# Repeating B for a group's first tile earlier on TensorE, and wider spacing of three small attention steps

## What the reference computes

```
def step(h, inp):                       # layers 0 and 1, 4096 steps, 4 orders, 192 channels, 16 states
    u_t, dt_t, B_t, C_t = inp
    h = jnp.exp(dt_t[..., None] * A) * h + (dt_t * u_t)[..., None] * B_t[:, :, None, :]
    y = jnp.einsum('bkdn,bkn->bkd', h, C_t)
    return (h, y)

attn = jnp.einsum('bhnd,bhmd->bhnm', q, k) * D ** (-0.5)     # layers 2 and 3: no softmax
y = jnp.einsum('bhnm,bhmd->bhnd', attn, v)
return y.transpose(0, 2, 1, 3).reshape(B, N, E) @ Wff + bff
```

## Time and profile before

| what | value |
|---|---|
| median of 3 runs | 11526.75 us (11501.28 to 11531.94) |
| profiled execution | 11522.77 us, its span 11520.9 us |
| DVE busy | 10175.8 us (88%) |
| POOL busy | 9737.9 us (85%) |
| PE busy | 8853.6 us (77%), granted clock 0.739 on average |
| ACT busy | 6996.5 us (61%) |

### The profile page before, as it was taken

One profiled execution on the slowest core, in us unless ns is written; L12 is line 12 of the kernel. 1 busy time (PEld: TensorE's weight loads), 2 busy tenths in 40 slices (PEclk: granted clock), 3 DMA queues, 4 the chain that ended last, 5 costly groups with the idle time before them and its releaser, 6 DMA issues.

```text
span 11520.9 us, 94504 instructions
## 1 busy us (share of the span) xinstructions
PE 8853.6 (77%) x26272; PEld 2221.2 (19%) x26272; DVE 10175.8 (88%) x6086; ACT 6996.5 (61%) x10714; POOL 9737.9 (85%) x4231
## 2 busy tenths in 40 slices
PE   6876677876888667869777787788788877777757
PEld 2211111211112111212112121122111221122213
DVE  3899998999889998989999899899988999898873
ACT  4665555665556555667556765566755666567654
POOL 3899988899888998989988888888888888998860
PEclk8875577875778667769677796788677876777766
DMA  3666688666775565655776668956687565665550
GB/s 100 143 136 135 140 154 153 150 136 142 159 154 147 131 159 148 157 131 142 171 157 146 133 149 151 161 146 141 137 162 150 140 151 138 160 159 120 123 137 14
DMA packets 1781801, 1631.73 MB, mean 142 GB/s; under 512 B 1323982, under 2 KB 1325296, under 8 KB 1781276
## 3 DMA queue, kind: packets, MB, share of 16 engines
q1 hardware_dynamic: 1781276, 1625.69, 63.9%
HBM read 625.58 MB, written 194.51 MB: 71 GB/s over the span
## 4 chain that ended last, share of the span: by engine, by line
PE 22%; DVE 21%; issue 20%; POOL 20%; ACT 8%; SPq 4%; DMA 3%; DVEq 0%; POOLq 0%; ACTq 0%
POOL pr L1645 14%; DVE hs L1566 9%; DVE ps L1551 7%; DVE hs L1562 4%; PE ps L1032 4%; PE ps L861 3%; PE ps L826 3%; PE ps L1019 3%; PE ps L1010 2%; POOL bup L1659 2%; PE ps L994 2%; POOL dur L1659 2%; POOL us L1636 2%; ACT dec L1289 2%; SPq L720 1%
## 5 line engine op out<-in xcount | busy, mean ns | idle before, releaser
L1645 POOL TENSOR_TENSOR pr<-hs,crep 128x1024 f32<-128x1024 f32 x3072 | 7184.8, 2355 | 1202.5 <-PE ps L1032 587.2
L1566 DVE TENSOR_TENSOR_SCAN hs<-dec,carry,ps 128x1024 f32<-128x1024 f32 x1728 | 4054.2, 2346 | 232.6 <-POOL pr L1645 7.0
L1551 DVE TENSOR_TENSOR ps<-ps,dur 128x1024 f32<-128x1024 f32 x2304 | 2789.4, 1211 | 524.1 <-PE ps L1019 384.0
L1019 PE MATMUL ps<-sbc,selb 96*128 96x512 bf16 x4608 | 1842.0, 492 | 1788.5 <-DVE hs L1566 1240.2
L1289 ACT ACTIVATE dec<-dtr,ac 128x1024 f32<-128x1024 f32 x2304 | 2610.7, 1136 | 436.5 <-DVE hs L1566 424.4
L1032 PE MATMUL ps<-pr,red 128*32 128x512 f32 x12288 | 2288.3, 828 | 25.4 <-POOL pr L1645 20.1
L1296 ACT ACTIVATE carry<-hs 128x1 f32<-128x1 f32 x2304 | 457.0, 199 | 2422.7 <-DVE hs L1566 2249.5
L1566 DVE TENSOR_TENSOR_SCAN hs<-dec,zero,ps 128x1024 f32<-128x1024 f32 x576 | 1351.3, 2346 | 84.7 <-ACT dec L1289 14.6
L826 PE MATMUL ps<-xb,tapw 96*96 96x512 f32 x2304 | 1184.8, 636 | 54.4 <-ACT sd L1122 51.9
L1019 PEld LDWEIGHTS ps<-sbc,selb 96*128 96x128 bf16 x4608 | 381.6, 108 | 3922.4 <-DVE hs L1566 2304.2
L1289 ACT ACTIVATE ps<-dtr,ac 128x1024 f32<-128x1024 f32 x768 | 848.3, 1105 | 399.3 <-DVE hs L1566 399.3
(11 more groups left out here) (227 smaller groups left out, 7621.3 us busy)
## 6 DMA issues: line engine op xcount, KB each, us to landing
dtr<-de SPq DMA_DIRECT2D x768, 512.0 KB, 7.9
dur<-us SPq DMA_DIRECT2D x768, 512.0 KB, 8.6
crep<-bc_d SPq DMA_DIRECT2D x512, 512.0 KB, 6.6
ust<-u_d SPq DMA_DIRECT2D x256, 384.0 KB, 6.0
y_d<-yst SPq DMA_DIRECT2D x768, 128.0 KB, 3.5
sd<-y_d SPq DMA_DIRECT2D x448, 192.0 KB, 5.2
brep<-bc_d SPq DMA_DIRECT2D x128, 512.0 KB, 5.8
u_d<-sd SPq DMA_DIRECT2D x64, 384.0 KB, 3.2
```

The source lines that it names most:

```text
L1019: mm = pe.matmul(ps[:, SLOT + 2 * (n % RS) + hf, :], selb[:, i % GT // 2, :], sbc[:, w % 2, B * hf:B * (hf + 1)], start=True, stop=True)
L1551: dve.tensor_tensor(slot(n), slot(n), dur[:, 2 * (G % 2) + i % 2, :], ALU.mult).then_inc(bu_v, 1)
L1566: dve.tensor_tensor_scan(hs[:, n % RH, :], dec[:, others(n) % RD, :], slot(n), init, ALU.mult, ALU.add).then_inc(scan_v, 1)
L1645: pool.tensor_tensor(pr[:, n % RP, :], hs[:, n % RH, :], crep[:, q, :], ALU.mult).then_inc(prod_g, 1)
```

## The change

There are two edits. On PE, the `fill` of a group's first tile stood at the head of the eighth tile's turn, behind the two ticks of the seventh. Now it stands in the seventh tile's turn, behind `reduce2` and ahead of that tile's two ticks. In the attention, PE's second small product comes one tick later, DVE's first copy one tick and its second copy two ticks later; the steps behind them keep their ticks.

```
@@ PE, attn
                 pe.matmul(ps[0:CH, SB, 0:CH], tbd, wff[:, l, :], start=True, stop=True).then_inc(mid_p, 1)
                 yield
+                yield
                 pe.wait_ge(mid_v, 3 * N + 2)
                 pe.matmul(ps[0:CH + 1, SB + 1, 0:CH], wq[:, l, :], mm_, start=True, stop=True).then_inc(mid_p, 1)
-                yield
                 yield
@@ PE, the loop over tiles
-                    if n + 1 < W * NT and not on_pool(n + 1):
+                    if n + 1 < W * NT and not on_pool(n) and not on_pool(n + 1):
                         fill(n + 1)
                     if i % 2 == 0 and n >= 4:
                         reduce2((n - 4) // 2)
+                    if n + 2 < W * NT and on_pool(n) and on_pool(n + 1):
+                        fill(n + 2)
                     for tick in (2 * i, 2 * i + 1):
```

## The result

The changed kernel takes 11610.2 us, median of 5 runs (11589.1 to 11627.5); the kernel before, run beside it, 11526.75 us. The ratio is 1.0076, with a 95% interval of 1.006 to 1.0092: slower by 83 us, where 11514 us and "no change that can be measured" were forecast. The profiled execution has a span of 11623.2 us, 102.3 us more than before.

What follows compares the result with a forecast made beforehand. DVE's own work was taken as the floor, its idle time as what order can change. The terms, 11522.8 - 48 + 26 + 15 - 3 = 11512.8 us, were given as 11514 us, with an 80% range of 11450 to 11575.

Steps and rivals of the forecast that it cites:

- The gain at first tiles: A group's first-tile `fill` (fill 1) starts earlier, right behind `reduce2` or the seventh scan: 83 groups win 103.8 us together.
- What the move costs: held side work: PE's side work in the seventh tile's two ticks now stands behind fill 1, delaying second tiles' `inp`: +26 us.
- fill 2's share of the gain: Fill 2, the second tile's `fill`, comes no earlier, so DVE waits there; 64 of 103.8 us are left.
- rival 3: TensorE's clock falls behind PE's idle time, so held work runs at the lower level: 11546 to 11609 us, chance 0.08.
- Its own test for that rival: The forecast is wrong if the mean granted clock moves from 0.739 by more than 0.02.
- rival 2: Held work decides: each held tick delays all that follows on PE; 11570 us at 30%, 11611 at 45%; chance 0.14.
- What waits behind the held ticks: DVE's side steps that read products of PE's two held ticks wait, 22 steps at 0.7 us each: +15 us.
- POOL's slack hides a late `reduce2`: The next group's `reduce2` comes up to 1.9 us later, but POOL's 1202.5 us idle hides its product's wait.
- Later tiles: Part of the gain is lost at waits for `fill` on tiles two to six: a quarter, 16 us, by choice.
- The attention's steps: Wider spacing of PE's and DVE's small attention steps takes most of DVE's waits there away: -3 us.
- all but vanish: Sign expected in the changed profile: DVE's waits for L940 and L937, in the attention, nearly disappear.
- The range: The forecast's 80% range for the changed kernel's time: 11450 to 11575 us.

## Why the prediction was wrong

**The bound and the gain were right.** All of it is DVE's idle time. The gain at first tiles was worked out at 103.8 us for 83 group ends, and at these it is 103.7; the kernel with the early `fill` there alone has it too.

**The step that failed** is "What the move costs: held side work", +26 us. It moved the held work behind `fill` at the speed that it had in the trace of before, at which two sums take 1.9 us. In 74 groups the work there now runs at the lower clock, and not only the held work: all that stands between the seventh scan and fill 2. At the place shown the held work is 2.1 us and fill 2 is 6.9 us later. Together with fill 2's share of the gain (40 us) the forecast for second tiles was +66 us; it is +144.5. Of this, 52.5 us are at the 83 group ends that win, against the 40, and 92.0 us at the other 300, against the 26: the held work was priced at less than a third of what it cost. The prediction had this mechanism as rival 3, at 11546 to 11609 us, and gave it 0.08. It had the parts: PE's idle time in one piece, 0.57 in an idle stretch, twice the time for a fill. It lacked the counting: what PE's idle time ahead of each fill 1 becomes (448.9 to 722.5 us in all, 4.80 us at a time), and which level was granted behind waits of such a length elsewhere in the same trace. That can be read there: from the seventh scan to the end of fill 2 the clock averages 0.60 at the 124 group ends where PE had idled 2 us or more ahead of fill 1, and 0.82 at the 224 where it had idled less than 1 us. Its own test for that rival, the mean clock moving by more than 0.02, would have missed it: it moved by 0.007, while that of the stretches behind the waits moved by 0.049.

**How much is clock and how much is order.** Of the 0.76% lost, zero matmuls at 55 places give back 0.38%, some 44 us. By where it lies in the profile, this is loss that the change had made. The other 0.38% is open between clock and order: it arises mostly where no zero matmuls stand, and there the clock is as low as in the change. Of it the experiments show only that it comes with held ticks: `fill` between the ticks, with one tick held less, is level with the kernel before. As far as it is order, it is rival 2 in kind. Which share of it is on which wait is read from one profile each and was not taken apart by a run.

**What waits behind the held ticks**, +15 us: the kind is right and the size is off. DVE's side steps idle 41.3 us more. L1519, L1471 and L1502 make 29.4 of it. The prediction took 0.7 us for 22 steps, with the products at the faster spacing.

**Not priced**: the scans' waits for POOL and ACT, +38.5 us. The prediction held that POOL's slack hides a late `reduce2`. POOL's products wait 793.6 us for `reduce2`, where it was 587.2, and DVE's recurrences wait 22.6 us at L1568 for POOL's products and 24.0 us at L1564 for its `dur`, where they waited 7.0 and 9.0. POOL's idle time as a total did not tell what it can hide at these groups.

**Later tiles**, +16 us by choice: they wait 21.2 us less. A delay at the second tile is probably also slack for the third; no run takes this apart.

**The attention's steps**, -3 us: waits for L937 and L941 are 6.7 us where they were 4.3, and the edit alone changes nothing; an error of no weight; that they "all but vanish" was wrong.

**The range** reached to 11575 us and missed. Rivals 2 and 3 held 0.22 between them, and both add in the same groups, since the held work is what runs slowly; they were treated as alternatives. That the top figure of each (11611 and 11609 us) lies at the measured time is luck and decides nothing: each reaches it alone, with the other at zero.

**Slips in the working**, too small to change the outcome. In the trace of before 93 first tiles wait for `fill`, 191.3 us, where the prediction has 95 and 195.9. The terms sum to 11512.8 us, and 4 us more is 11516.8, not 11514. Rival 2 makes the kernel slower once 13% of its 276 us comes through (36 us, by the same sum), not over 40%. And the 276 us are the time from the end of `reduce2` to the end of the held work or of the seventh scan; PE is busy for 189 us of it.

## What to carry to other kernels

An in-order wait moved ahead of ready work costs that work twice: it comes later, and if the engine is TensorE it may then run at half the clock, with all that is queued behind it, as here. So before moving a matmul that waits, list for each place how long the engine would idle in one piece and what stands behind it up to the next consumer's deadline, and reprice that whole stretch at the lower level. And where a move wins at some places of a loop and loses at others, make it only where it wins: here the uniform move cost 0.76%, the same move at 15 places of 48 gained 0.32%.

## What the runs showed of the hardware

- After 4.80 us of idle time in one piece TensorE ran at 0.50 for the next 11 us, though it was busy for 10.90 of these 11.00 us. At the same place in three other scans it idled only 2.00 us, and the clock behind was 0.50 to 0.52 as well. After 1.24 us of idle, with 3.63 us of zero matmuls ahead, it ran at 1.00. How short a wait is harmless the runs do not say.
- Matmuls with zero weights can keep the clock up: 16 of 512 columns took 3.63 us of idle time, and 660 of them took the clock at 55 group ends to 0.926, where three profiles of the same order without them show 0.61 to 0.70 at 48 of these. Twelve were not always enough: at two of the eight ends of the worst place, with 2.10 us of idle behind them, the clock was still 0.54 and 0.52. And they are free only inside a wait: in the old order the same 660 put 57 us on first tiles.
- A higher mean clock does not by itself mean a faster kernel: 0.749 with the old order went with 1.0017, since what raised the clock also stood in the way of `fill`.
